# Two of GpSimd's low halves moved forward among its row writes, and a third given to VectorE, in the first MoE of a Macaron block

## The reference, cut to what matters

```
x = x + 0.5 * moe(layernorm(x))
x = x + sparse_attention(layernorm(x))     # 16 heads, top 32 keys of an indexer
x = x + 0.5 * moe(layernorm(x))
```

```
scores = softmax(x @ gate_w);  topk_w, topk_idx = top_k(scores, 2)
g      = silu(x @ w_gate[e]) * (x @ w_up[e])
routed = sum over the two chosen e of topk_w * (g @ w_down[e])
shared = (silu(x @ sw_gate) * (x @ sw_up)) @ sw_down        # hidden width 352
moe    = routed + shared
```

## Time and profile before

| | us |
|---|---|
| median of 3 runs (892.57 to 897.28) | 892.71 |
| the profiled execution | 894.12 |
| its span | 892.2 |
| PE busy | 867.7 (97%) |
| DVE busy | 670.5 (75%) |
| ACT busy | 553.4 (62%) |
| POOL busy | 399.1 (45%) |

### The profile page before, as it was taken

The page is one execution under the profiler, slowest core; times in us unless marked ns, Lnnn a source line. Parts: engine busy times, 40 slices in busy tenths (PEclk is TensorE's granted clock), DMA queues, the critical chain, the costliest instruction groups (busy, mean ns, idle before and its releaser), DMA issues.

```text
span 892.2 us, 18848 instructions
## 1 busy us (share of the span) xinstructions
PE 867.7 (97%) x5705; PEld 778.8 (87%) x5705; DVE 670.5 (75%) x2361; ACT 553.4 (62%) x1615; POOL 399.1 (45%) x531
## 2 busy tenths in 40 slices
PE   9998999999999999999999999999999999999997
PEld 5777899888897899998999998999989998789996
DVE  7775669678898987776787776878577675757786
ACT  6764455567665777776666766767467675435562
POOL 0587688300001333433333444555348685136672
PEclk9998999999999999999999999999899999999999
DMA  9255995550001110100000001998001033634474
GB/s 348 100 154 170 345 349 187 117 119 1 25 1 48 36 37 12 36 2 29 21 1 2 1 1 46 302 304 240 1 24 49 19 130 148 273 91 132 132 267 154
DMA packets 54514, 99.39 MB, mean 111 GB/s; under 512 B 5968, under 2 KB 38864, under 8 KB 52368
## 3 DMA queue, kind: packets, MB, share of 16 engines
q1 hardware_dynamic: 46736, 76.35, 26.6%
q0 software_dynamic: 7680, 21.83, 7.8%
HBM read 46.57 MB, written 51.60 MB: 110 GB/s over the span
## 4 chain that ended last, share of the span: by engine, by line
PE 47%; POOL 3%; DVE 2%; issue 1%; DMA 1%; ACT 1%; DVEq 0%; SPq 0%; POOLq 0%
PE ps L862 22%; PE ps L867 19%; PE ps L1114 3%; POOL SP L1974 2%; PE ps L1029 1%; PE ps L1000 1%; POOL xg L1928 1%; DMA RAW<-yr 1%; PE ps L905 0%; DVE RR L1394 0%; DMA yr<-FA,IDX 0%; DVE PA L1394 0%; DVE xl L1394 0%; ACT SP L1363 0%; DVE SP L1843 0%
## 5 line engine op out<-in xcount | busy, mean ns | idle before, releaser
L1974 POOL TENSOR_SCALAR SP<-SP,RC 128x128 f32<-128x128 f32 (+1 forms) x256 | 192.8, 771 | 244.8 <-DVE RC L1853 244.3
L1394 DVE TENSOR_TENSOR RR<-ps,RR 128x256 fp32r<-128x256 f32 (+2 forms) x322 | 157.6, 525 | 70.9 <-ACT RR L1158 69.7
L867 PE MATMUL ps<-RR,RA 128*128 (+1 forms) x894 | 165.0, 322 | 7.7 <-POOL RR L1906 3.6
L1363 ACT ACTIVATE SP<-SP,NB 128x128 f32<-128x128 f32 (+1 forms) x256 | 113.5, 444 | 68.4 <-DVE NB L1843 68.1
L1158 ACT ACTIVATE RR<-ps 128x256 fp32r<-128x256 f32 (+2 forms) x322 | 137.4, 469 | 28.1 <-PE ps L862 24.9
L867 PEld LDWEIGHTS ps<-RR,RA 128*128 128x128 f32 x894 | 131.7, 191 | 14.4 <-issue 12.4
L862 PE MATMUL ps<-xh,RR 128*128 128x512 f32 x368 | 132.6, 404 | 0.0
L1803 DVE SCALAR_TENSOR_TENSOR PA<-R,IW,PA 128x128 f32<-128x128 f32 x240 | 84.8, 415 | 28.2 <-ACT R L1355 28.0
L1942 POOL DMA_INDIRECT yr<-FA,IDX x78 | 84.1, 1078 | 46.4 <-DVE FA L1729 16.9
L867 PE MATMUL ps<-RR 128*128 128x256 f32 x768 | 104.4, 286 | 0.0
L867 PEld LDWEIGHTS ps<-RR 128*128 128x128 f32 x768 | 97.8, 193 | 1.2 <-DVE RR L1394 0.7
(11 more groups left out here) (249 smaller groups left out, 1800.6 us busy)
## 6 DMA issues: line engine op xcount, KB each, us to landing
xg<-stage SPq DMA_DIRECT2D x15, 1161.0 KB
FA<-xg SPq DMA_DIRECT2D x78, 129.0 KB
kept<-RR SPq DMA_DIRECT2D x8, 1216.0 KB
RR<-kept SPq DMA_DIRECT2D x8, 1216.0 KB, 12.2
X<-yr POOLq DMA_DIRECT2D x6, 512.0 KB, 6.1
RAW<-yr SPq DMA_DIRECT2D x6, 512.0 KB, 5.1
RAW<-wex_in SPq DMA_DIRECT2D x8, 352.0 KB, 8.5
RAW<-wsh_in SPq DMA_DIRECT2D x6, 384.0 KB, 8.2
```

The source lines that it names most:

```text
L867: return e.matmul(o, a, c, start=start, stop=stop, skip_group_check=True)
L1363: ins = e.activation(SP[:, k, i, o:o + w], SP[:, k, i, o:o + w], ACT.Exp, scale=-1.0, bias=NB[:, k, 2 * i + z:2 * i + z + 1], accum_out=SM ...
L1394: return e.tensor_tensor(o, p, q, alu)
L1974: ins = e.tensor_scalar(SP[:, k, i, o:o + w], SP[:, k, i, o:o + w], RC[:, k, 2 * i + z:2 * i + z + 1], None, ALU.mult)
```

## The change

Three steps change place in the hand-written list. The first two low halves of GpSimd move two row writes forward, behind the sixth and the tenth write. The fourth, of part 0 of expert 3, leaves GpSimd (where it stood behind the 24th write) and goes to VectorE, between the second batch's "count" and "place". No operation is added or removed.

```diff
-    yield from [("count", 0, 0, 6), ("place", 0, 0, 6), ("choose", 0, 0)] + marks(0, 0, 1) + first[:8] + rest(parts[0])
-    yield from first[8:13] + rest(parts[1]) + first[13:] + rest(parts[2])
+    yield from [("count", 0, 0, 6), ("place", 0, 0, 6), ("choose", 0, 0)] + marks(0, 0, 1) + first[:6] + rest(parts[0])
+    yield from first[6:11] + rest(parts[1]) + first[11:] + rest(parts[2])
...
-    yield from part_of("tm", 4) + [("raise", 0, 1), ("count", 0, 1, 6), ("place", 0, 1, 6), ("choose", 0, 1)] + marks(0, 2, 3)
-    yield from spread(0, 2, 0) + spread(0, 3, 0) + rest(parts[3]) + [("tag", 0, 2)] + spread(0, 2, 1) + [("index", 0, 0), ("index", 0, 1)]
+    yield from part_of("tm", 4) + [("raise", 0, 1), ("count", 0, 1, 6)] + low(parts[3]) + [("place", 0, 1, 6), ("choose", 0, 1)] + marks(0, 2, 3)
+    yield from spread(0, 2, 0) + spread(0, 3, 0) + [("tag", 0, 2)] + spread(0, 2, 1) + [("index", 0, 0), ("index", 0, 1)]
```

## The result

The changed kernel takes 891.62 us (median of 20 runs, 889.14 to 895.55), the kernel before 894.16 beside it (20 runs, 890.25 to 897.28). The ratio is 0.9974, with a 95% interval of 0.9963 to 0.9984: 2.3 us less, between 1.4 and 3.3 (the two medians alone are 2.5 apart). That is within 0.5%, and real. Forecast were 1.4 less from a base of 892.71, which gave 891.3.

The account below looks back on a forecast made before the run. PE bounds the kernel, with a second path, GpSimd, then SyncE, then DMA, setting the pace from about 85 us. −1.67 + 0 + 0 + 0.3 = −1.4 us from 892.71 gave 891.3 us, range 889.1 to 893.8.

Parts of the forecast that it names:

- Step 1: GpSimd's queue: without the fourth low half, everything issued behind it comes 1.67 us earlier.
- Step 2: GpSimd's first two low halves move two row writes forward; nobody wants the delayed writes: 0 us.
- Step 3: VectorE makes the fourth low half before place, 0.88 us, covered by a 1.40 us wait for the count: 0.
- Step 4: GpSimd and VectorE collide: selection products up to 1.6 us late, hidden by PE; row write beside new low half +0.3.
- Step 5: PE's first routed product starts 2 to 3.6 us earlier; PE then waits at tile 9, gaining 1.4 at tile 12.
- The sum: Terms −1.67, 0, 0 and +0.3 make −1.4 us, carried by GpSimd and DMA from 106 to 146, then PE.
- PE leads: Rival, chance 0.16: second path less tight, PE keeps its 3.6 us and the clock, 6.4 in all: 886.3 us.
- half way: Middle case of PE leads: the slack at tile 9 is kept, 1.4 + 1.5 = 2.9 us gained: 889.8 us.
- Hidden anyway: Rival, chance 0.24: GpSimd or the DMA queues lose the early gain again before 146 us: 892.5 us.
- Slower: Rival, chance 0.08: pause moves to tile 9, clock falls there, costing 2.8 us of PE time: 893.8, up to 895.
- The change not as said: Rival, chance 0.02: new low half misses VectorE's wait, place late, first fetch slips up to 0.8: 891.3 to 892.
- everything behind 100 us shifted by one constant near 1.4: Sign in the trace: all behind 100 us shifts alike, near 1.4 us; differing shifts at 100 and 150 refute it.

Follow-up runs that it names:

- useless work: Changed kernel plus a GpSimd subtraction that nobody reads where its fourth low half stood, made once or twice: 0.9988 once, 1.0001 twice, against the kernel before.
- second profile: The changed kernel run and profiled once more, no edit: 891.13 us, 0.9968 against the kernel before.
- the late store: SyncE's first 1.2 MB store moved behind tile 9's fetch: 0.9976 in the changed kernel, 1.0003 in the one before, both against the kernel before.

## Why the forecast was right

**What bounds the kernel.** "Behind PE stands a second path, GpSimd, then SyncE, then DMA": right in its head. GpSimd's queue carries most of the gain, shown by useless work that takes it away again and by a further low half removed that adds as much again; the useless work also costs PE 2 us, which it had in hand at tile 9. The bound on the gain was right too: not the 3.6 us of PE's wait, though that wait is gone and PE starts 5.2 us earlier. The middle link, that PE's standing at tile 9 hands the time on, fell: fetch 9 made 2 us earlier by another way brought nothing. So did the link at tile 12, for which PE was said to wait for the fetch already. The earlier trace rows put that pause of 0.58 down to "issue", not to the fetch, and the changed kernel's second profile has no wait there, which was one of the prediction's own signs of being wrong. Which later point of the GpSimd chain hands it on (the result writes, or the saturated stretch behind them) no run took apart.

**Step 1**, −1.67: measured −1.63, at index 0 and at the first result write alike. That it agrees to 0.04 is luck, since index 0 came at 73.54, 74.31 and 74.46 in three profiles with GpSimd's four low halves, and at 72.28 to 72.83 in five of the changed order. The means are 1.58 apart.

**Step 2**, the moves cost 0: with the moves alone 1.0004 [0.9992, 1.0016]. The second low half found its source at 42.67. Together with step 3 they did a little good that nobody had forecast: without them a row write begins inside VectorE's low half and takes 0.46 more.

**Step 3**, VectorE's low half costs 0: its 0.88 was exact, and it costs no time. The reason given was not: the wait of 1.40 us was in the one execution shown, and in the profile after place stands right behind the low half. What covers it is the rest of the step, that VectorE's queue had nothing to lose there, and that everything ahead of it was earlier: the two small products began at 41.94, where it was 43.69 in before, and place still came at 45.79, before 46.10.

**Step 4**, the collisions. The first one came: two products held until GpSimd was through, 2.53 us. It struck the pair behind the sum, not the product at 42.77 that the step named, because in the new profiles VectorE was ahead of the execution shown. So it did not make "selected" late, as the step had it: the sum that releases PE's count starts at 41.86, before the held pair, and the count's matmuls begin at 42.41. What was held is VectorE's own queue, up to its low half and place, and the end moved by nothing, as said.

The second, +0.3 for the write beside VectorE's low half, didn't come: 0.98, because the write had started first. The mean of 0.34 was no price for one low half. By the single records a write that begins inside a VectorE low half ends 0.83 to 0.87 us behind it, or behind the whole run of them, and one that begins earlier is not held; so the price here was 0 or 0.46 (1.43 with the fourth low half alone), by which of the two starts first.

The rule of the Trainium skill, "SBUF — State Buffer", section "SBUF: two separate sides", a lock held for the whole instruction by whichever engine starts first, fits the end of VectorE's products against GpSimd's low half to within 0.1 us (44.47 against 44.38). Their recorded starts are the other way round (42.13 against 42.67), so the trace does not show that GpSimd was first. For the other direction, a row write beside a VectorE operation, both rows agree with it: the write that started first shows no hold, and the one that started inside does.

**Step 5**, PE. The forecast had hidden 0 at 65.87 or 67.5; it starts at 64.25. The profile of before has one more pause of PE ahead of it, 1.71 us at 38.81, where the others have 0.33, and the count was not late. Fetch 9 was to go at 83.9 and went at 83.31 and 82.90, tile 9 stood for 3.68 and 3.08 (2 to 3.5 forecast). What the step left out is that an early PE brings something of its own: put on the line of the table, before's index 0 of 74.46 would give −0.6 and not 0, and the 73.54 of the late store in before −1.5. With the queue's share, 1.6 or 0.7 by the same two profiles, either gives about the 2.3 measured. How it divides comes from single profiles and is inside the error, so this is a reading and not shown.

**The sum**, −1.4, stands at the end of the measured interval (−1.4 to −3.3). The terms that made it small were the +0.3 and the missing share of PE. That 891.3 lies only 0.3 from the measured 891.62 is partly luck: the base was 1.45 too low (892.71, the median of three runs, against 894.16 of twenty), and the gain 0.9 too small.

**The rivals.** PE leads (889.8 for half way): no; PE was 5.2 us early and the time 2.3 less. The half way's price, 2.9, is what the second measurement gave, but not by its mechanism: the slack won at tile 9 is worth nothing by the late store. Hidden anyway: no, by the same interval and by the useless work that costs what it takes. Slower, the pause moves and takes the clock: its mechanism came in full, a pause of 3.68 and 0.86 of the clock in 80 to 92, and its price did not; with the pause filled and the clock at 1.00 the time is no better. PE had more in hand there than the 0.3 to 1.5 us of the rival: turning tile 12 another 1.1 us earlier changed nothing. The change not as said: place came at 45.79 against 45.02 with the moves alone, 0.77 late for a low half of 0.88, and nothing followed.

**Of the signs**, "everything behind 100 us shifted by one constant near 1.4" could not be read from one profile: by the first activation at about 180 us the two profiles of the changed kernel differ by 3.5 us, more than the whole effect.

## What to carry to other kernels

Where a slow instruction stands in the queue of an engine with two jobs, look at what is queued behind it before looking at who waits for it: here the wait for its result (3.6 us of PE) was worth some 0.6 to 1.5 us, ±1.2, and its own 1.7 us in the queue the rest. Then the next question is how many more can be moved: the second low half given to VectorE brought about another 2 us. The third brought nothing, because the row writes became longer by what it had taken, and the fourth made the queue shorter again for no time. Work moved from one engine to its neighbour is to be priced by what starts inside it there, not by a mean. And useless work put in to tell two causes apart can touch both: look at what it holds. An effect of 2 us is to be read from medians and from edits that undo it; one profile against one profile has an error as large, and a wait that only one execution shows is no cover to count on.

## What was not expected of the hardware

A fall of the granted clock behind a pause of 3 to 4 us cost nothing here: 0.86 in 80 to 92 us, against 1.00 when the pause was filled with 14 matmuls (3.17 us), with 2.3 and 1.3 us less than before. The same fall at tile 0 (0.57 over 6.5 us) could not be told from the pause that made it.

GpSimd and VectorE hold each other, in both directions. VectorE's small products ended with GpSimd's low half (rows of 2.53, 2.52 and 2.59 us in three kernels, 0.42 without). And a row write that began inside a VectorE low half was held, where a write alone takes 0.97: it took 1.43 with the fourth low half alone, 1.45 and 1.54 with three on VectorE. In the fourteen profiles, up to 84 us, 69 row writes begin inside a low half, more than 0.035 us behind its start and 0.14 before its end. Of these 55 end 0.83 to 0.87 us behind that low half, and the other 14 are those of the next paragraph. Six that begin within 0.035 us of the start took 0.96 to 0.98.

The write of 3.10 us at 57.33 is the same thing. It begins inside a run of four low halves, which ends at 59.59, and it ends at 60.43, 0.84 behind. The row of the run:

```profile
56.91 2.68 DVE L1394 TENSOR_TENSOR RR<-RAW,RR 128x704 fp32r<-128x704 f32 x4
```

In each of the fourteen profiles the write in that place ends 0.83 or 0.84 behind the run, also where it began later and took 2.64 (58.16 in before with the late store). Why this write waits for all four low halves, and those at 53.99 and 61.99 only for the one that they began in (0.85 and 0.83 behind it), no row shows.

So work taken from GpSimd doesn't always shorten its queue: three low halves gone and two gone gave the same index 0 (70.67 and 70.36), with 1.74 us more in the row writes.
